# Moving the full attention's exponential and log to the head of ScalarE's slot in a fused hybrid transformer block

## The reference

```python
# attention a: causal with a distance bias
scores = einsum(q, k) / sqrt(8) + where(k <= q, -(q - k), -1e30)
out_a = softmax(scores) @ v @ w_out.T + b_out
# attention b, first step: full softmax over all 512 keys, used only to rank the tokens
scores = softmax(einsum(q, k) / sqrt(8))
entropy = -sum(scores * log(clip(scores, 1e-8)));  max_attn = scores.max(-1);  influence = scores.sum(-2)
importance = -0.4 * mean(entropy) + 0.3 * mean(max_attn) + 0.3 * mean(influence)
idx = top_k(importance, 51)
# second step: a small attention over 51 picked keys and 64 compressed ones
out_b = softmax(q @ [k[idx], compress(k)] / sqrt(8)) @ [v[idx], compress(v)] @ Wo
# feed-forward
y = (silu(x @ wg.T) * (x @ wu.T)) @ wd.T
```

## Time and profile before

| what | value |
|---|---|
| median of 3 runs | 1777.08 us (1765.18 to 1785.22) |
| the profiled execution: its time, its span | 1775.59 us, 1773.8 us |
| busy over the span: PE, DVE, ACT, POOL | 1368.7, 1266.5, 1021.9, 535.6 us |
| granted TensorE clock, mean | 0.73 of full |
| the full attention's exponentials: count, first and last start | 512, 301.0 and 1614.3 us |

### The profile page before, as it was taken

The page is one execution under the profiler, slowest core; times in us unless marked ns, Lnnn a source line. Parts: engine busy times, 40 slices in busy tenths (PEclk is TensorE's granted clock), DMA queues, the critical chain, the costliest instruction groups (busy, mean ns, idle before and its releaser), DMA issues.

```text
span 1773.8 us, 26884 instructions
## 1 busy us (share of the span) xinstructions
PE 1368.7 (77%) x7981; PEld 607.2 (34%) x7981; DVE 1266.5 (71%) x3771; ACT 1021.9 (58%) x2550; POOL 535.6 (30%) x964
## 2 busy tenths in 40 slices
PE   1377797788768878888888888887888788787565
PEld 0132343234233333443344334433443242243232
DVE  1330432996788798989897989798878789877221
ACT  1024145577547766867586768676777657745132
POOL 3020232254124522442334234423341334212021
PEclk9555556577758776978797879788877768857566
DMA  2201103102302220223023201220111102100100
GB/s 53 45 19 26 25 25 79 24 2 58 69 3 48 49 64 3 48 56 62 5 46 62 57 11 41 62 50 16 24 38 32 24 7 63 19 12 15 24 14 6
DMA packets 69881, 61.39 MB, mean 35 GB/s; under 512 B 12088, under 2 KB 67432, under 8 KB 69736
## 3 DMA queue, kind: packets, MB, share of 16 engines
q1 hardware_dynamic: 69736, 59.68, 16.4%
HBM read 41.19 MB, written 18.27 MB: 34 GB/s over the span
## 4 chain that ended last, share of the span: by engine, by line
PE 38%; DVE 26%; issue 13%; ACT 11%; DMA 4%; POOL 4%; SPq 1%; DVEq 0%; ACTq 0%; POOLq 0%
DVE junk L1042 7%; PE bank L1373 5%; ACT setup L882 4%; PE bank L1273 4%; PE bank L1337 4%; DVE negs L1143 3%; PE bank L1315 3%; PE bank L1398 3%; DVE nm L982 2%; PE bank L1293 2%; ACT pT L860 2%; DVE nml L988 2%; PE bank L1365 2%; DMA k_stacks<-part_dram 2%; PE bank L1408 2%
## 5 line engine op out<-in xcount | busy, mean ns | idle before, releaser
L882 ACT ACTIVATE setup<-negs,nmB 128x512 f32<-128x512 f32 x512 | 367.0, 717 | 235.6 <-DVE negs L1143 224.4
L720 POOL TENSOR_TENSOR thr<-nmB,lnZ 128x1 f32<-128x1 f32 x512 | 150.1, 293 | 880.8 <-ACT lnZ L886 872.3
L1042 DVE SCALAR_TENSOR_TENSOR junk<-negs,thr,setup 128x512 f32<-128x512 f32 x512 | 410.0, 801 | 0.8 <-POOL thr L720 0.5
L1143 DVE TENSOR_SCALAR_CACHE_REDUCE negs<-bank 128x512 f32<-128x512 f32 x512 | 349.5, 683 | 35.8 <-PE bank L1365 35.2
L860 ACT ACTIVATE pT<-bank 128x512 f32<-128x512 f32 x320 | 188.6, 589 | 193.6 <-PE bank L1323 192.8
L1365 PE MATMUL bank<-k_stacks,q_stacks 48*128 48x512 bf16 x512 | 234.6, 464 | 30.8 <-DVE negs L1143 18.9
L1315 PE MATMUL bank<-q_stacks,k_stacks 55*128 55x384 bf16 (+3 forms) x512 | 149.5, 358 | 65.3 <-ACT pT L860 65.2
L1373 PE MATMUL bank<-setup,rz 128*1 128x512 f32 x1024 | 189.6, 824 | 1.5 <-DVE rz L1161 1.5
L982 DVE TENSOR_REDUCE nm<-bank 128x4 f32<-128x512 f32 x128 | 87.8, 686 | 98.8 <-PE bank L1289 98.8
L1293 PE MATMUL bank<-k_stacks,q_stacks 52*128 52x384 bf16 (+2 forms) x384 | 97.0, 344 | 64.1 <-DVE nml L989 45.6
L994 DVE TENSOR_REDUCE nm<-bank 128x4 f32<-128x460 f32 x128 | 81.1, 634 | 81.1 <-PE bank L1408 81.0
(11 more groups left out here) (195 smaller groups left out, 2424.1 us busy)
## 6 DMA issues: line engine op xcount, KB each, us to landing
part_dram<-part SPq DMA_DIRECT2D x16, 768.0 KB, 3.6
q_stacks<-part_dram SPq DMA_DIRECT2D x192, 64.0 KB
k_stacks<-part_dram SPq DMA_DIRECT2D x192, 64.0 KB
s_stacks<-part_dram SPq DMA_DIRECT2D x48, 128.0 KB
x<-in_L_attn_a_x_dram SPq DMA_DIRECT2D x16, 256.0 KB, 2.9
x_dram<-x SPq DMA_DIRECT2D x8, 256.0 KB, 2.2
x<-x_dram SPq DMA_DIRECT2D x8, 256.0 KB, 2.7
out_dram<-x SPq DMA_DIRECT2D x8, 256.0 KB, 2.5
```

The lines of the kernel that those rows point to most:

```text
L720: pool.tensor_tensor(thr[mb % 2][:, h, t:t + 1], nmB[mb % 2][:, h, t:t + 1], lnZ[mb % 2][:, h, t:t + 1], ALU.subtract).then_inc(s_bt, 1)
L882: act.activation(E[:, n % NE, :], negs[n % NS][:, :], ACT.Exp, scale=-1.0, bias=nmB[mb % 2][:, h, t:t + 1], accum_out=Z[mb % 2][:, h, t:t ...
L1042: dve.scalar_tensor_tensor(out=junk[:, :], in0=negs[n % NS][:, :], scalar=thr[mb % 2][:, h, t:t + 1], in1=E[:, n % NE, :], op0=ALU.min, op ...
L1143: dve.tensor_scalar(negs[n % NS][:, :], RING[n % RN][:, :], -1.0, None, ALU.mult, ALU.min, accum_out=nmB[mb % 2][:, h, t:t + 1]).then_inc( ...
```

## The change

In ScalarE's program for a slot, the block of the full attention's tile (exponential into `setup`, then `lnZ`) is put ahead of the block with the `pT` exponentials, the `p` exponentials and the heads' copy `leave`. Nothing is added or removed; the single steps stay last. The lines of what moved are now L859 (full exponential), L863 (`lnZ`), L874 (`pT`) and L883 (`p`).

```diff
                 for g in range(SLOTS):
                     now = own_slots(g)
-                    for b, a in now:
-                        for u in range(N2):
-                            if a == A2_AT[u // G2] + u % G2 + 1:
...
-                                act.wait_ge(s_full[4], count("a2", b, u))
-                                act.activation(pT[:, js[0]:js[0] + len(js), c * T:c * T + WIDTH[c]],
-                                               bank[4][:, :].rearrange("p (j q) -> p j q", j=len(js)),
-                                               ACT.Exp).then_inc(s_free[4], 1)
...
-                                act.activation(p2[h % HPQ][0:NK, :], bank[4][0:NK, :], ACT.Exp).then_inc(s_free[4], 1)
-                        for k in range(2):
-                            for j in range(NG):
-                                if a == LEAVE[k][j]:
-                                    leave(k, j, b)
-
                     m = main_tile(g)
                     if m:
...
                         act.activation(lnZ[mb % 2][:, h, t:t + 1], Z[mb % 2][:, h, t:t + 1], ACT.Ln, scale=CLIP
                                        ).then_inc(s_bz, 1)
+
+                    for b, a in now:
+                        for u in range(N2):
+                            if a == A2_AT[u // G2] + u % G2 + 1:
...
+                        for k in range(2):
+                            for j in range(NG):
+                                if a == LEAVE[k][j]:
+                                    leave(k, j, b)
```

More of the change, by code:

```diff
@@ L851, in _ @@
                     now = own_slots(g)
+                    m = main_tile(g)
+                    if m:
+                        mb, h, t, n = m
+                        act.wait_ge(s_bm, n + 1)
+                        if n >= NE:
+                            act.wait_ge(s_bn, n - NE + 1)
+                            act.wait_ge(s_bi, (n - NE) // NT + 1)
+                        act.activation(E[:, n % NE, :], negs[n % NS][:, :], ACT.Exp, scale=-1.0,
+                                       bias=nmB[mb % 2][:, h, t:t + 1],
+                                       accum_out=Z[mb % 2][:, h, t:t + 1]).then_inc(s_be, 1)
+                        act.wait_ge(s_be, n + 1)
+                        act.activation(lnZ[mb % 2][:, h, t:t + 1], Z[mb % 2][:, h, t:t + 1], ACT.Ln, scale=CLIP
+                                       ).then_inc(s_bz, 1)
                     for b, a in now:
@@ L873, in _ @@
                                     leave(k, j, b)
[L875 to L887, removed]
                     for b, a in now:
```

## The result

The changed kernel takes 1868.67 us (median of 4 runs, 1859.44 to 1873.05) against 1775.13 us for the kernel before in the same comparison: 1.052 times as long, 95% interval 1.0445 to 1.0595. Slower was forecast, but by 23 us, and it is 93. The measured time lies outside the range.

The account below looks back on a forecast made before the run. No engine was full; DVE and PE were taken to drive each other, with ScalarE between. The terms 7 + 9 + 4 - 10 - 5 - 2 + 20 gave +23 us, 1799 us; range 1755 to 1840 us.

Parts of the forecast that it names:

- The path: ScalarE to PE: later `pT` and `p` delay PE's second-pass scores, then full scores and DVE's copy two slots on.
- the last term of the sum: PE off the chain: 105 tiles 0.95 us late, 100 us, of which a fifth reaches DVE: +20 us.
- its upper bound: PE off the chain: all lateness of the 105 tiles shows, 100 us.
- The other terms: Chain crossings through ScalarE and DVE's reciprocal: 7 + 9 + 4 - 10 - 5 - 2 us.
- A gain by `lnZ` to GpSimd: Chain from ScalarE's `lnZ` to GpSimd's `thr`, 21 times: -10 us, bounds -20 and 0.
- The price where DVE leads: `pT` ends 2.27 us after the copy's start, PE wants bank 4 at 1.90: 0.4 us late per slot.
- Much slower: Rival, chance 0.10: most of the 100 us shows, 1850 us and over; PE's clock may fall too.
- its first mechanism: Much slower rival: waits on `pT` come in slots where DVE later runs dry, showing most of the 100 us.
- the sign that it and not the order carries the difference: Main stretch: a granted clock moved by over 0.03 would mean the clock carries the difference.
- Faster: Rival, chance 0.20, under 1759 us: PE is the late one, so ScalarE does the full exponential while awaiting bank 4.
- No change: Rival, chance 0.33, 1760 to 1794 us: PE's new lateness is swallowed by its own waits for DVE.
- a slack of 5.1 - 4.1 us over two slots: Loop from `negs` through ScalarE and PE back to `negs`: spans 5.1 us, needs about 4.1.

Follow-up runs that it names:

- the two traces at 0.74: Kernel before with PE's second-pass scores right behind the full scores (1862.63 us), and with the full scores ahead of the second-pass scores (1783.5 us).
- tie_only: Kernel before, order kept, but ScalarE's slot begins with a wait for its own slot's `negs`: 1819.83 us, ratio 1.0273.
- after_double: Changed kernel with the first-pass score matmuls of bank 3 issued twice: 1929.47 us, ratio 1.0934.
- before_double: Kernel before with the first-pass score matmuls of bank 3 issued twice: 1849.5 us, ratio 1.0414.

## Why the prediction was wrong

- **The path was right, and its price wrong.** PE's waits for `pT` and `p` were to grow from 55.5 to about 150 us: 147.5. ScalarE's wait for PE ahead of `pT` was to shrink well below 108.6: 45.8. Its wait for `negs` was to grow beyond 224.4: 410.9. DVE's reciprocal: 10.2 to 2.0 us. The stretch ahead of the full attention kept its length; the one behind it, which was to keep its own, grew by 7 us.
- **The step that failed** is the last term of the sum: PE's lateness off the chain, 105 tiles x 0.95 = 100 us, of which "I take a fifth: +20 us". The loss came out near its upper bound. PE's waits for DVE gave up 39 us where I counted on 96 as cover (26 of them in the items that I had named), and DVE stood 95 us longer where 20 to 40 were forecast. The fifth came from the share of slots in which DVE waits for PE now. That share describes the kernel before; the change made PE late in slots in which DVE had not waited for it.
- **The bound itself was met partly by luck.** It is 105 waits of the kernel before, each 0.95 us longer. In the changed kernel there are more waits, too: PE's weight loads stand 195 times for `pT` or `p` in the main stretch where they stood 134 times, for 247.0 us where it was 121.9. The tiles for which PE had not waited had no term in the sum, though their `pT` comes later as well.
- **The clock had no term** in the sum, only in a rival. The main stretch's clock fell by 0.05 and PE's busy time grew by 69 us. That such a loss comes without a lower clock too is shown by the two traces at 0.74; the clock's own part of the 93 us stays open.
- **The other terms** together were to give +3 us. They are not resolved one by one. A gain by `lnZ` to GpSimd is not resolved either: the chain leaves that way 14 times where it did so 21 times. Besides the reciprocal, ScalarE ends one more of DVE's gaps in the kernel before (`rzw` for `s_stacks`, 0.6 us), too little to matter.
- **The price where DVE leads** (2.27 against 1.90 us) was too kind. tie_only, whose path is 1.3 us by the same reckoning, should have been nearly free and cost 41 us.
- **The rivals.** *Much slower*, at 0.10, is what happened, by its first mechanism at least: 1869 us lies in its 1850 and over. The clock passed the 0.03 that I had named as the sign that it and not the order carries the difference. By the traces at equal clock that sign says too much: the order costs time by itself. The mechanism deserved the larger chance, but not because PE stands ready nearly each time: rows 5 and 6 show 129 waits of weight loads for 343 tiles. *Faster* needed more slots with a late bank 4 than with a late `negs`; rows 4 spoke against it and did so rightly. *No change* relied on a slack of 5.1 - 4.1 us over two slots. That a mean slack does not protect a ring in which single steps stand unevenly is my reading; no run varied it.

## What to carry to other kernels

When two waits stand in one in-order queue, the instruction that another engine waits for through a single buffer should not stand behind the one that waits for the busiest engine: work alone ahead of it cost 12 us here, a wait alone 41, and both 93. Where such a reader has to be late, look at what stands behind the waiting instruction on the other engine; moving the next tile's independent matmul ahead of it gave back 73 of 93 us. Do not discount new lateness by the share of slots in which its consumer waits today: the new order changes who waits. And read the clock in the stretch where the time was lost, not over the whole span, before you clear it or blame it.

## What the runs showed of the hardware

The mean clock of an execution can move by what happens outside the stretch in question: ahead of the full attention it was 0.97 in after_double and 0.59 in before_double, which gives the first the higher mean (0.757 against 0.719) although its main stretch had the lower clock (0.73 against 0.77). Executions of the changed kernel have 0.687, 0.691, 0.744 and 0.749 and times within 14 us of each other, so a difference of 0.06 in this mean says little about the time. In the main stretch the clock was 0.77 before the change and 0.72 with it; what lowered it is not shown.
